# Weighted sine sums of four attention units moved from VectorE to TensorE, with new orders of work

## What is computed

```python
# x: (32, 64, 256)
y = einsum('bnh,boh->bno', x, W[itok7]) + b[itok7]         # per-item projection, one of 8
q, k, v = heads(y @ Wq.T + bq), heads(y @ Wk.T + bk), heads(y @ Wv.T + bv)   # 16 heads of 16
sim = q @ k.T / sqrt(16) / (abs(temperature) + 0.1)
scores = sum(alpha[:, f] * sin(2*pi*sim/freq[f] + phi[:, f]) for f in range(5))
w = sigmoid(scores); w = w / (sum(w) + 1e-10)
x = x + layernorm((w @ v) @ Wo.T + bo) * gamma + beta
h = x + relu(x @ W1[itok8] + b1) @ W2[itok8] + b2          # per-item adapter, one of 10
h = layernorm(h) * gamma[itok8] + beta[itok8]
for t in range(32):                                        # over the items
    i, f, g = sigmoid(h[t] @ wi.T + c @ ui.T + bi), sigmoid(...), tanh(...)
    c = f * c + i * g                                      # c: (64, 256)
out = x + tanh(h @ wo.T + c @ uo.T + bo)
```

## Time and profile before

| | us |
|---|---|
| median of 3 runs | 343.79 (341.45 to 344.33) |
| the profiled execution, own time | 344.01 |
| span of its profile | 342.2 |
| VectorE busy | 292.0 (85%) |
| TensorE busy (matmuls) | 281.7 (82%) |
| ScalarE busy | 270.4 (79%) |

### The profile page before, as it was taken

One profiled execution on the slowest core, in us unless ns is written; L12 is line 12 of the kernel. 1 busy time (PEld: TensorE's weight loads), 2 busy tenths in 40 slices (PEclk: granted clock), 3 DMA queues, 4 the chain that ended last, 5 costly groups with the idle time before them and its releaser, 6 DMA issues.

```text
span 342.2 us, 7110 instructions
## 1 busy us (share of the span) xinstructions
PE 281.7 (82%) x2532; PEld 166.5 (49%) x2532; DVE 292.0 (85%) x633; ACT 270.4 (79%) x405; POOL 31.8 (9%) x42
## 2 busy tenths in 40 slices
PE   5956679467659898899999998999988998998872
PEld 5745338334236755544466454454644454543351
DVE  2388986999998999999999999999999999564256
ACT  1297689998997999999999999999998864323124
POOL 5000200002020001030010201202011301110000
PEclk9998896858969999999999999999999999999987
DMA  5788046560563340025103430300330130000006
GB/s 167 223 251 313 2 71 191 110 178 1 138 164 104 48 117 2 0 65 126 14 13 62 115 80 0 81 14 7 88 95 2 28 99 1 2 0 0 2 12 233
DMA packets 27876, 27.54 MB, mean 80 GB/s; under 512 B 10434, under 2 KB 19778, under 8 KB 27842
## 3 DMA queue, kind: packets, MB, share of 16 engines
q1 hardware_dynamic: 27266, 26.46, 28.9%
q10 hardware_dynamic: 576, 0.64, 0.7%
HBM read 23.15 MB, written 2.10 MB: 74 GB/s over the span
## 4 chain that ended last, share of the span: by engine, by line
ACT 31%; DVE 29%; PE 18%; issue 9%; SPq 6%; POOL 3%; DMA 2%; DVEq 0%; ACTq 0%
ACT ang L1055 10%; DVE sc L1567 7%; ACT ang L1064 6%; DVE ang L1552 5%; PE pg L626 4%; PE pf L459 3%; SPq L312 3%; ACT gat L1105 2%; PE pr L578 2%; ACT sc L1046 2%; PE pf L481 2%; DVE fc L1703 2%; POOL rs L413 2%; ACT sc L1074 2%; DVE ang L1543 2%
## 5 line engine op out<-in xcount | busy, mean ns | idle before, releaser
L1567 DVE SCALAR_TENSOR_TENSOR sc<-ang,small,sc 128x512 f32<-128x512 f32 (+1 forms) x160 | 97.7, 638 | 1.0
L1064 ACT ACTIVATE ang<-ang,qs 128x2560 f32<-128x2560 int32 x32 | 77.0, 2425 | 0.5 <-DVE ang L1552 0.4
L1055 ACT ACTIVATE ang<-sc,phase 128x512 int32<-128x512 f32 (+1 forms) x126 | 72.4, 641 | 0.0
L617 PE MATMUL pg<-gate_w,zT 128*64 128x384 f32 x256 | 50.6, 500 | 1.3 <-DVE zT L1693 1.1
L626 PE MATMUL pg<-gate_u,cT 128*64 128x384 f32 x256 | 47.9, 495 | 3.5 <-DVE cT L1712 3.4
L1552 DVE TENSOR_SCALAR ang<-ang 128x2560 int32<-128x2560 int32 x32 | 47.2, 1487 | 0.1
L1105 ACT ACTIVATE gat<-pg 128x384 f32<-128x384 f32 x32 | 15.5, 485 | 27.6 <-PE pg L626 27.6
L1543 DVE TENSOR_SCALAR ang<-sc,phase 128x256 int32<-128x256 f32 (+1 forms) x74 | 27.7, 411 | 6.1 <-ACT sc L1046 6.0
L539 PE MATMUL pf<-qm,kT 64*64 64x128 f32 x512 | 19.9, 299 | 10.5 <-DMA qm<-qT 3.4
L626 PEld LDWEIGHTS pg<-gate_u,cT 128*64 128x64 f32 x256 | 16.3, 136 | 24.8 <-issue 15.2
L617 PEld LDWEIGHTS pg<-gate_w,zT 128*64 128x64 f32 x256 | 15.1, 136 | 20.3 <-issue 15.2
(11 more groups left out here) (111 smaller groups left out, 431.8 us busy)
## 6 DMA issues: line engine op xcount, KB each, us to landing
wc<-in_cond SPq DMA_DIRECT2D x30, 257.0 KB, 3.1
w<-in_up SPq DMA_DIRECT2D x32, 128.2 KB, 2.6
wa<-in_down SPq DMA_DIRECT2D x32, 66.0 KB, 2.1
xt<-in_xt SPq DMA_DIRECT2D x8, 256.0 KB, 2.8
xg<-in_x SPq DMA_DIRECT2D x3, 512.0 KB, 5.2
qm<-qT SPq DMA_DIRECT2D x48, 32.0 KB, 2.1
out_t<-go SPq DMA_DIRECT2D x6, 256.0 KB, 2.1
gate_w<-in_gate_w SPq DMA_DIRECT2D x1, 768.0 KB, 6.9
```

The lines of the kernel that those rows point to most:

```text
L617: pe.matmul(pg[n % 2][u * L:(u + 1) * L, 0:GCOLS], zT[:, q % 2, kc, t * L:(t + 1) * L], gate_w[:, kc, u, :], start=False, stop=(kc == KC - ...
L1055: op = act.activation(ang[:, n % SLOTS, f, r], unit(n)[:, r], ACT.Identity, scale=TURN / FREQS[f], bias=phase[:, p * NF + f:p * NF + f + 1])
L1064: act.activation(a.bitcast(F32), a, ACT.Sin, scale=2 * PI_LOW / TURN, bias=qs[:, 3:4]).then_inc(sine_ready, 1)
L1567: op = dve.scalar_tensor_tensor(out=unit(n)[:, r], in0=sine, scalar=amp, in1=unit(n)[:, r], op0=ALU.mult, op1=ALU.add)
```

## The change

- The sums of units 4, 5, 6 and 7 (the head pairs 0 to 3 of group 1) are made by TensorE: for each of the five frequencies one matmul of a 128 x 128 diagonal matrix holding alpha with the 128 x 512 sine tile, accumulated in gate bank pg0 or pg1, in turn. ScalarE's sigmoid reads the bank. Their twenty `add_sine` calls are gone.
- VectorE makes twenty diagonals (`diagonals(4)` to `(7)`, 128 x 128 each) in buffers that are not in use yet.
- `first_biases` waits for weights(7) and stands behind it.
- ON_ACT of units 5 and 7 goes from 4 to 3: one angle of each goes from ScalarE to VectorE.
- All lists are in new orders, SyncE's too. No other call is added or removed; the lists now hold 19 table loads, because `sines` and `weights` alternate more often. Helpers for moves by DMA and for held outputs are added but their lists of quarters are empty.

```diff
-ON_ACT = [2, 2, 3, 3, 3, 4, 3, 4, 3, 4, 3, 4, ...
+ON_ACT = [2, 2, 3, 3, 3, 3, 3, 3, 3, 4, 3, 4, ...
-SUMMED = 0
+SUMMED = (4, 5, 6, 7)
+SUM_PAIRS = (0, 1, 2, 3)
...
         def diag(p, f):
-            k = (p - pairs_of(0)[0]) * NF + f
-            home = go if k < 4 * (NQ - 2) else x1
-            return home[:, k // 2 % (2 * (NQ - 2)), k % 2 * P:k % 2 * P + P]
+            k = SUM_PAIRS.index(p) * NF + f
+            home = go[:, 2 + k // 2] if k < 20 else x1[:, 8 + (k - 20) // 2]
+            return home[:, k % 2 * P:k % 2 * P + P]
...
             def summed(n):
                 pe.wait_ge(sine_ready, n + 1)
-                pe.wait_ge(diag_ready, n + 1)
-                wait(pe, w_ready, n - 1)
+                pe.wait_ge(diag_ready, SUMMED.index(n) + 1)
+                k = SUMMED.index(n)
+                if k > 1:
+                    pe.wait_ge(w_ready, SUMMED[k - 2] + 1)
                 for p in pairs_of(n):
                     r = pair_in(n, p)
                     for f in range(NF):
-                        mm = pe.matmul(pg[n % 2][:, r], diag(p, f), ang[...], start=(f == 0), stop=(f == NF - 1))
+                        mm = pe.matmul(pg[k % 2][:, r], diag(p, f), ang[...], start=(f == 0), stop=(f == NF - 1))
                 mm.then_inc(sum_done, 1)
```

ScalarE's list where units 4 to 12 are worked, cut to its sines and sigmoids and what shows their places:

```diff
             weights(3, False)
-            first_biases()
...
             sines(4, True)
-            sines(5, False)
+            turned(0)
             angle(6, 2)
...
+            sines(5, False)
...
             squares(0)
+            weights(4, True)
+            weights(5, False)
             angle(9, 1)
             angle(9, 2)
+            sines(6, True)
...
+            sines(7, False)
+            sines(8, False)
...
             sines(9, False)
             sines(10, False)
-            sines(11, False)
-            weights(4, True)
-            weights(5, False)
+            queries(2, 0)
+            weights(6, True)
             angle(11, 1)
             angle(11, 2)
+            keys(2, 0)
+            weights(7, False)
             queries(2, 1)
+            first_biases()
...
             weights(8, False)
             weights(9, False)
-            weights(10, False)
...
+            sines(11, True)
...
             gates(0)
+            weights(10, True)
             angle(12, 4)
+            weights(11, False)
+            sines(12, True)
```

More of the change, by code:

```diff
@@ L114, in last_unit_in, with count @@
     return max((m + 1 for m in range(FIRST[g]) if unit_at(m) < hi and unit_at(m) + UCOLS > lo), default=0)
+def count(parts, q):
+    return sum(k <= q and k % 2 == q % 2 for k in parts)
 def wait(eng, sem, value):
@@ L776, in _ @@
             condition(6, 0)
+            turn_residual(1)
             condition(6, 1)
+            adapter_down(1)
+            turn_tokens(3)
+            input_gates(3, 0)
             state_turned(1)
-            turn_residual(1)
+            adapter_up(1)
             state_gates(2)
-            adapter_down(1)
+            turned(2)
+            queries(3, 0)
+            state_turned(2)
+            input_gates(3, 1)
+            state_gates(3)
+            keys(3, 0)
+            turn_normed(1)
@@ L1651, in adapted @@
             def adapted(q):
-                dve.wait_ge(base_ready, q + 1)
+                if q in BASE_BY_DMA:
+                    dve.wait_ge(base_moved[q % 2], 16 * count(BASE_BY_DMA, q))
+                else:
+                    dve.wait_ge(base_ready, sum(k not in BASE_BY_DMA for k in range(q + 1)))
                 dve.wait_ge(up_done, q + 1)
@@ L1891, in _ @@
             add_sine(13, 3)
+            cell_step(1, 1)
+            conditioned(3)
+            state_copy(1)
+            add_sine(13, 4)
             add_sine(14, 0)
[L1893 removed]
             add_sine(14, 1)
[L1895 to L1896 removed]
+            adapted(1)
             add_sine(14, 2)
+            cell_step(2, 0)
+            moments(1, 0)
+            cell_step(2, 1)
             add_sine(14, 3)
[L1899 removed]
+            state_copy(2)
@@ L1922, in _ @@
-            shifted_language(1)
-            cell_step(3, 0)
+            angle(18, 0)
+            add_sine(16, 2)
+            wrap(17)
+            shifted(3)
+            cell_step(4, 0)
+            angle(18, 1)
+            cell_step(4, 1)
+            wrap(18)
+            state_copy(4)
+            add_sine(16, 3)
+            add_sine(17, 0)
+            add_sine(17, 1)
+            angle(19, 0)
+            add_sine(17, 2)
+            add_sine(17, 3)
+            add_sine(18, 0)
+            hidden(2, 0)
```

1126 lines of the change are left out of this document (548 added, 578 removed).

## The result

The change makes the kernel slower, by 1.6%. Median 349.43 us (347.47 to 350.97, 4 runs) against 343.77 before; the ratio is 1.0162, 95% interval 1.0108 to 1.0216. The prediction was 339.9 us, range 335.5 to 346.3.

The account below looks back on a forecast made before the run. VectorE and ScalarE were taken as both full, the time set by the last sum plus a tail. From 344.0 us profiled, -2.0 (last sum) and -1.9 (tail) gave 340.1, less 0.2 to the median: 339.9, range 335.5 to 346.3.

Parts of the forecast that it names:

- part 2: ScalarE up to sines(31): 10.1 us more work, 0.9 gained at the start, 6.2 of idle time gone; ends at 278.4.
- ScalarE keeps its idle time: Rival for ScalarE's queue: it waits as long as today, sines(31) at 284.6, total 346.1 us; chance 0.12.
- Part 3: Last sum on VectorE: 5.6 us behind sines(31), at 284.0, 2.0 us earlier; the limit has moved to ScalarE.
- Part 5: TensorE's twenty matmuls, 17.2 us at full clock: taken as 0, up to +13 if at half clock.
- Part 1: VectorE's work: 13.6 us of sums less, 0.9 of angles and 2.7 of diagonals more, net 10.0 us less.
- Part 4: Tail behind the last sum: state_gates(23) ahead of turned(7), so state_gates(24) starts at 10.4 us, not 12.3: -1.9.
- Part 6: Loads: spread_q(1, 1) starts nearly 2 us sooner but is hidden by unit 4's sines: 0.
- the serial end: From state_gates(24) on: eight serial steps and the output, forecast to follow unchanged.
- the 0.2 that the forecast took off: Whole kernel: the profiled execution stood 0.2 us above the runs' median, so 340.1 became 339.9.
- the two slow cases: Rivals: ScalarE's idle time stays, 346.1 us, chance 0.12; TensorE becomes the limit between 60 and 110, 345.9, 0.10.
- the switches: Rival on ScalarE: a switch costs twice its row, six new ones 7.9 us more, 347.8; chance 0.01.

Follow-up runs that it names:

- e5: Changed kernel's lists up to group 1's end, with the order of the kernel before behind it (17 loads): 348.0 us, ratio 1.0113.
- e15: Changed kernel with the order of the kernel before between group 1's end and the last quarter: 350.19 us, ratio 1.0179.
- e14: Kernel before with the changed kernel's lists from the last quarter on, state_gates(23) ahead of turned(7), 13 loads: 346.63 us, ratio 1.0085.
- e2: Changed kernel with tanh for the sigmoid of the weights and no table load after the first: 344.64 us, ratio 1.001.
- e18: Changed kernel run once more, unchanged, for a second profile: 349.86 us, ratio 1.0152.
- e3: Kernel before with tanh for the sigmoid of the weights and no table load after the first: 344.73 us, ratio 1.0014.
- e4: Kernel before, order unchanged, with six more loads of the table set already in place: 347.98 us, ratio 1.0108.
- e6: Kernel before up to group 1's end, with the changed kernel's order behind it (15 loads), no sum on TensorE: 347.67 us, ratio 1.0089.
- e7: Kernel before's lists with units 4 and 5 summed on TensorE, four more angles to VectorE, 13 loads: 347.05 us, ratio 1.0111.
- e10: Kernel before's lists with units 4 and 8 summed on TensorE, weights(8) and first_biases behind weights(7), 13 loads: 344.07 us, ratio 0.9976.
- e11: Kernel before's lists with unit 8 alone summed on TensorE, weights(8) and first_biases behind weights(7), 13 loads: 343.27 us, ratio 0.9982.
- e12: e11 with group 2's queries and keys earlier: 344.05 us, ratio 0.9971.
- e16: e11 with tanh for the sigmoid of the weights and no table load after the first: 342.53 us, ratio 0.9951.
- e1: Changed kernel with weights(29) moved behind sines(31), two table loads less: 354.85 us, ratio 1.0331.
- e9: Changed kernel with one matmul in each of the four sums, not five: 348.21 us, ratio 1.0117.
- e13: Changed kernel with tanh for the weights' sigmoid, no load after the first, and one matmul a sum: 345.05 us, ratio 1.0043.

## Why the prediction was wrong

**The step that failed is in part 2:** "Of the 7.9 us of idle time in 54 to 276, much is waiting for VectorE or for what VectorE feeds", so that 6.2 of it goes. The idle time came out at 7.2, where 1.7 was forecast. That is 5.5 of the 6.0 us by which sines(31) was late on its forecast (284.4 for 278.4). Only 1.9 of the 6.9 us that the view of waits explains were for VectorE, and these did fall, to 0.5; 5.0 were for TensorE, and 4.7 are so again, 1.5 of them for a sum that the change itself put there. VectorE's slack, the reason given for the 6.2 us, was there in group 1 only: up to 121 us ScalarE's idle time fell from 3.7 to 1.9, and from there to 276 us, where VectorE is nearly as full as before (3.6 us idle for 1.6), it rose from 4.2 to 5.3. ScalarE's seven waits for TensorE there, 3.3 us in all, each stand behind a wait of TensorE for VectorE (cell_step or residual_added), so "what VectorE feeds" names them rightly; but VectorE had nothing to give. The work was right: 10.1 us more, 0.9 of it gained at the start, makes 9.2, and by the windows ScalarE is busy 9.5 us more between 54 us and the end of sines(31). A slack of one stretch was carried to all of them; the view of waits and VectorE's windows would have told.

This was the slow rival, "ScalarE keeps its idle time", at 0.12: sines(31) at 284.6, and 284.36 came. It was the right rival for this part. Its 346.1 is still 3.3 us short of the median: the rest is in parts 3 and 5 and in the order of VectorE's list.

**Part 3 failed with it.** "The limit has moved to ScalarE" is true up to 121 us (64.86 of 66.80) and false behind it: VectorE is busy for 167.38 of 171.0 us. The last sum came 7.5 us behind sines(31), not 5.6, since VectorE still had three adds of unit 30 to do, where one was forecast, and a division.

**Part 1** had the saving about right up to group 1's end (9.4 less busy, 1.8 of it work left for later), but took it for time won. The diagonals cost 4.1 us, not 2.7: the end of the bound that I had not taken. And one cost had no term: the order of VectorE's list. Work left over from group 1, wrap(13) and angle(13, 0), is 1.8 us by its rows (e5, which keeps it in the old order, takes 1.9 more), cell_step(21, 1) and state_copy(21) 0.4 as forecast. Neighbours of which the second starts about 0.03 us behind the first, where most overlap by 0.08, are 33 from group 1's end to the last sum where before had some 18; 10 of them, for 3 before, are adds that follow each other on the same sum (the expectation of e15 took all 15 more for adds). The lost overlap of 15 such pairs is 1.2 us of busy time, an estimate; their gaps are 0.5 of the 2.0 us more idle time. Most of the rest is in the view of waits: in before VectorE waited 1.0 us in this stretch for GpSimd's roots (rs), in after 2.4, ahead of residual and normalise:

```profile
DVE stage L1716 <- POOL rs L428: 1.5, 2, 0.9
DVE x L1664 <- POOL rs L428: 0.9, 2, 0.6
```

1.8 + 0.4 + 1.2 + 2.0 = 5.4, of 5.8 measured.

**Part 4** was right in its place (9.6 us for a forecast of 10.4), but it is no gain of state_gates(23)'s move: alone (e14) that loses. By the profiles it is bought with the 2.1 us of the middle order (e15).

**Part 5**, 0 with up to +13, was right for the clock in the first profile and some 1.5 us too low in three of the five of this stretch, where summed(4) ran partly at half clock. scores(6) ended at 105.0 in the first, not 103: from 49.7 to 105.0 TensorE worked 48.3 us and waited 7.0, for 46.6 and 7 in the forecast. In the first, ScalarE's wait of 1.5 us for a sum ahead of its sigmoid was its longest. e2 shows how little room TensorE had (3.9 us idle once the loads were gone).

**Part 6**, 0, is not contradicted: the one new wait for a load that stands out, 1.1 us of VectorE for xt at 55 us, lies in a stretch where VectorE idles anyway.

**The sum.** From 339.9 to the profile's 347.5 there are 6.0 us of sines(31), 1.9 of part 3, -0.8 of part 4, 0.3 in the serial end (44.3 us for 44.0) and the 0.2 that the forecast took off. The other 2.0 to the median are not in this profile; e18's, at 351.4, has them and more. Two slips in the prediction's own figures change nothing: a third of the two slow cases and the switches is 0.08, not 0.10, and the forecast's range is given once as 338.7 to 341 and once as 338.5 to 341.5.

Of the switches: e3's nothing, e4's 3.8 and e2's 4.8 us show that a load has no price of its own. By its row it holds ScalarE for 1.31 us; six cost half of 7.8 where both engines are full, and thirteen gave back nothing. The Trainium skill (ScalarE: Activation LUTs, "What ACT_TABLE_LOAD costs") gives about 2.66 us for every switch to a different set, which for six is an estimate of 16.0 us. e4's six loads switch no set, so that run does not test it. The rows of after do, and don't bear it out: a sine that ends at 277.77 is followed by the load at 277.79 and the sigmoid at 279.08, 1.31 us.

**What stays open.** How much of the 5.7 us between the medians is in group 1 and how much behind: the two profiles of after say +0.2 and +2.0 for group 1, +5.8 and +6.8 behind it, -2.3 and -2.2 in the tail. With the five profiles of the new lists up to group 1's end (71.3 in the mean) and the two of the old (70.2), it is about +1.1, +6.3 and -2.2, an estimate that comes to 5.2. The 2.0 us of idle time behind group 1 were read from the trace and not taken away one by one; nor does a run separate the two loads that the new order adds there from its other costs. An order that keeps the old middle and has the recurrence ahead at the end was not tried.

## What to carry to other kernels

Where two engines are both full and feed each other, relief of one becomes its idle time; ask of every moved microsecond what the other engine, and the queue that takes the work, has free in that same stretch, and read it from the list of what each engine waited for, not from a mean rate of idle time. Cut the profiles of both kernels at the same marks before comparing them: here three marks showed at once that the stretch relieved was not shorter and that most of the loss lay behind it, in an order changed along with it. Take more than one profile where the clock changes between executions. A reordered list is a cost of its own: on VectorE count the neighbours that depend on each other, and on TensorE what stands behind each wait.

## What the runs showed of the hardware

- scores(2) ends between 48.4 and 52.9 us in the profiles, and between 50.7 and 52.9 in four kernels that are the same up to there (before, e4, e6, e14). Behind group 1 seven kernels of one order (before, e3, e7, e10, e11, e12, e16) agree within 0.3 us over 165.
- TensorE's granted clock differs between executions of one program: 1.00 and 0.92 in 54 to 104 us of after, with the same wait of 1.83 us ahead of scores(4) in both; e1, e5 and e15, with the same lists there, have 0.94, 0.91 and 0.94. With fewer matmuls it was lower (e9 0.79; e13 0.84 for e2's 0.93), so that in e9 14 us less work at full clock shortened TensorE's busy time by 5.5 us against the first profile of after and by 7.5 against the second.
- Loads of a table set that is in place already (e4) take the same 1.283 us as real switches.
